# Gathers of a graph kernel held to the matrix engine's steps, and its last stage with logarithm roots and four buffers

## The reference

```python
x = _layernorm(x + _L0_gnn_ref(x, edge_index, edge_attr_16, ...))
x = _layernorm(x + _L1_gnn_ref(src, dst, x, edge_attr_3, ...))
```

```python
d = gelu(layer_norm(gelu(layer_norm(x3 @ Wd1 + bd1)) @ Wd2 + bd2))
logits = w1[target] - w2[source] + d
e = jnp.exp(logits - seg_max[target])
a = e / segment_sum(e, target)[target]
out = segment_sum(a * (w3[source] + d), target)
```

## Time and profile before

| | |
|---|---|
| median of 3 runs | 2032.91 us (2018.93 to 2034.91) |
| the profiled execution | 2048.31 us |
| its span, first to last instruction | 2046.5 us |
| stage dense | about 25 to 720 us |
| stage weigh | about 720 to 870 us |
| stage first | about 870 to 1275 us |
| stage dist | about 1275 to 1413 us |
| stage second | about 1413 to 2046 us |
| granted PE clock, mean of the execution | 0.823 |

### The profile page before, as it was taken

One profiled execution on the slowest core, in us unless ns is written; L12 is line 12 of the kernel. 1 busy time (PEld: TensorE's weight loads), 2 busy tenths in 40 slices (PEclk: granted clock), 3 DMA queues, 4 the chain that ended last, 5 costly groups with the idle time before them and its releaser, 6 DMA issues. The chain is left out here.

```text
span 2046.5 us, 22495 instructions
## 1 busy us (share of the span) xinstructions
PE 1446.2 (71%) x5771; PEld 832.8 (41%) x5771; DVE 1575.8 (77%) x3462; ACT 744.6 (36%) x1570; POOL 1053.9 (51%) x1154
## 2 busy tenths in 40 slices
PE   5787787877788600588888882786777667766773
PEld 4555555555555400133333331674333233333331
DVE  2788777778788668578888783685888888878886
ACT  2676666666677500122322221453211111111111
POOL 3566556666567300025545556002576767776764
PEclk9899898889899755677777775687988988888886
DMA  2455545445555510101111111001211222222120
GB/s 80 129 179 160 163 150 167 150 145 162 161 167 168 120 51 0 38 25 43 42 43 47 41 36 31 4 4 25 46 43 48 44 51 47 48 53 46 48 48 13
DMA packets 163175, 156.87 MB, mean 77 GB/s; under 512 B 84789, under 2 KB 105404, under 8 KB 163049
## 3 DMA queue, kind: packets, MB, share of 16 engines
q1 hardware_dynamic: 131048, 125.34, 20.0%
q0 software_dynamic: 32000, 30.10, 7.6%
HBM read 71.30 MB, written 73.65 MB: 71 GB/s over the span
## 5 line engine op out<-in xcount | busy, mean ns | idle before, releaser
L416 POOL DMA_INDIRECT dense_pairs<-in_x_dram,gix x400 | 418.4, 1046 | 278.9 <-PE bank L460 135.9
L442 PE MATMUL twin<-AC,dense_hb 128*128 128x256 f32 x784 | 219.4, 429 | 93.5 <-DVE dense_hb L594 67.4
L1438 POOL DMA_INDIRECT out_dram<-second_orow,second_stage x200 | 199.5, 998 | 71.1 <-issue 53.2
L1430 POOL DMA_INDIRECT second_pairs<-x_table,second_stage x200 | 203.8, 1019 | 59.2 <-issue 54.4
L954 POOL DMA_INDIRECT x_table<-first_xr,first_stage x200 | 202.3, 1011 | 54.0 <-issue 53.7
L442 PEld LDWEIGHTS twin<-AC,dense_hb 128*128 128x128 f32 x784 | 158.3, 213 | 127.8 <-DVE dense_hb L594 74.8
L948 POOL COPY first_stage<-first_rows 128x4 int32<-128x4 int32 x50 | 10.0, 200 | 310.8 <-DVE first_xr L1148 175.4
L995 PE MATMUL twin<-first_zb,Mstack 128*64 128x512 f32 x400 | 158.9, 885 | 0.0
L1079 DVE TENSOR_TENSOR first_zb<-twin,XT 128x512 f32<-128x512 f32 x200 | 130.8, 686 | 23.1 <-PE twin L987 14.7
L434 PE MATMUL bank<-dense_xT,Mblk 128*128 128x512 f32 x196 | 115.2, 672 | 34.9 <-ACT dense_xT L530 21.7
L987 PE MATMUL twin<-first_wt,headsel 24*128 24x512 bf16 x200 | 74.3, 498 | 81.0 <-DMA first_mask<-mask_rows 37.4
(11 more groups left out here) (270 smaller groups left out, 3603.0 us busy)
## 6 DMA issues: line engine op xcount, KB each, us to landing
dense_rows<-in_x_dram SPq DMA_DIRECT2D x98, 256.0 KB
x_table<-dense_xr SPq DMA_DIRECT2D x98, 256.0 KB
out_dram<-dense_orow SPq DMA_DIRECT2D x98, 256.0 KB
XT<-dense_turned SPq DMA_DIRECT2D x50, 256.0 KB
dense_pairs<-in_x_dram,gix POOLq DMA_INDIRECT x400
target_rows<-first_xr SPq DMA_DIRECT2D x50, 128.0 KB
second_pairs<-target_rows SPq DMA_DIRECT2D x50, 128.0 KB
second_mask<-mask_rows SPq DMA_DIRECT2D x50, 128.0 KB
```

The lines of the kernel that those rows point to most:

```text
L416: pool.indirect_dma_start(out=pairs[b][:, j % 4, F * (j // 4):F * (j // 4) + F], out_offset=None, in_=x, in_offset=bass.IndirectOffsetOnAx ...
L442: last = nc.tensor.matmul(pGC[b][:, j * 256:(j + 1) * 256], hb[b][:, j * 128:(j + 1) * 128], AC[:, :], start=True, stop=True)
L1430: pool.indirect_dma_start(out=pairs[u.off % 2][:, j, 0:F], out_offset=None, in_=x1, in_offset=bass.IndirectOffsetOnAxis(ap=stage[a][:, j:j ...
L1438: pool.indirect_dma_start(out=out, out_offset=bass.IndirectOffsetOnAxis(ap=stage[a][:, 4 + j:5 + j], axis=0), in_=orow[a][:, j, :], in_off ...
```

## The change

In **dense**, each of POOL's gathers now waits for one group of PE: gathers 0 to 3 and 4 to 7 of an edge unit belong to two following slots, and in slot k they wait for `project` of unit k-1, `turn_rows` of unit k, `rows_of_x` of unit k-3 and `rows_of_h` of unit k-2. These are the four groups of PE's slot k, in PE's order.

```diff
+                def after_matmuls(k, part):
+                    if part == 0 and k > 0:
+                        pool.wait_ge(p_made, min(k, DENSE))
+                    if part == 1:
+                        pool.wait_ge(xt_made, min(k + 1, DENSE))
+                    if part == 2 and k > 2:
+                        pool.wait_ge(x_rows_made, min(k - 2, DENSE))
+                    if part == 3 and k > 1:
+                        pool.wait_ge(gc_made, min(k - 1, DENSE))
...
                     for j in range(8):
+                        after_matmuls(2 * e + j // 4, j % 4)
                         pool.indirect_dma_start(
```

```diff
+                    def after_matmuls(u, part):
+                        if part == 0:
+                            atleast(pool, turned, u.count(-1))
+                        if part == 1:
+                            atleast(pool, fell_made, u.count(-2))
+                        if part == 2:
+                            atleast(pool, linear, u.count(-1))
+                        if part == 3:
+                            atleast(pool, rows_made, u.count(-2))
...
+                    def slot(u):
+                        o = u.back(5)
                         for j in range(4):
...
+                            if u.valid(UNITS):
+                                after_matmuls(u, j)
+                                gather(u, j)
+                            if o.valid(UNITS):
+                                if j == 0:
+                                    pool.wait_ge(out_made, o.count(1))
+                                scatter(o, j)
```

```diff
+                    def guess_inverse(u):
...
+                        act.wait_ge(rows_made, u.count(1))
...
+                        nc.scalar.activation(ln_den[:, :, :], sum_rows(u)[:, :, 0, :], ACT.Ln).then_inc(ln_den_made, 1)
...
+                        nc.scalar.activation(inv[:, :, :], ln_den[:, :, :], ACT.Exp, scale=-1.0).then_inc(inv_made, 1)
...
+                    def guess_roots(u):
...
+                        nc.scalar.activation(ve[:, :], s2[:, :], ACT.Identity, bias=eps1[:, :]).then_inc(ve_made, 1)
...
+                        nc.scalar.activation(ln[:, :], ve[:, :], ACT.Ln).then_inc(ln_made, 1)
...
+                        nc.scalar.activation(guess[:, :], ln[:, :], ACT.Exp, scale=-0.5).then_inc(guess_made, 1)
...
+                        nc.scalar.activation(halved[:, :], guess[:, :], ACT.Square, scale=0.5 ** 0.5).then_inc(halves_made, 1)
```

```diff
                     def divide(u):
+
                         dve.wait_ge(inv_made, u.count(1))
+                        atleast(dve, over_made, u.count(0))
+                        nc.vector.tensor_tensor(off[:, :, :], sum_rows(u)[:, :, 0, :], inv[:, :, :], ALU.mult).then_inc(off_made, 1)
+                        nc.vector.tensor_tensor(quo[:, :, :], sum_rows(u)[:, :, 1, :], inv[:, :, :], ALU.mult).then_inc(quo_made, 1)
...
+                        nc.vector.scalar_tensor_tensor(over[:, :, :], off[:, :, :], 2.0, quo[:, :, :], ALU.subtract, ALU.mult)\
+                            .then_inc(over_made, 1)
```

More of the change, by code:

```diff
@@ L1369, in gnn @@
                 sums = [sbp(f"sums{i}", [128, COLS]) for i in range(2)]
-                inv, quo = sbp("inv", [128, 4, F]), sbp("quo", [128, 4, F])
+                ln_den, inv, quo, off, over = (sbp(n, [128, 4, F]) for n in ("ln_den", "inv", "quo", "off", "over"))
                 res, sqr = sbp("res", [128, 4, F]), sbp("sqr", [128, 4, F])
                 cen = [sbp(f"cen{i}", [128, 4, F]) for i in range(2)]
-                orow = [sbp(f"orow{i}", [128, 4, F]) for i in range(2)]
-                mean, nmean, s2 = sbp("mean", [128, 4]), sbp("nmean", [128, 4]), sbp("s2", [128, 4])
@@ L1457, in slot @@
-                        stage_gather(u.back(-1))
-                        if o.valid(UNITS):
-                            scatter(o)
-                    slots(UNITS, 6, slot)
-                    for b in range(2):
-                        pool.wait_ge(scattered[b], 64 * (UNITS // 2))
+                        for j in range(4):
+                            if u.valid(UNITS):
[5 more added lines that the diff above has]
+                                scatter(o, j)
@@ L1465, in _, with sum_rows @@
+                    slots(UNITS, 5, slot)
+                    for b in range(4):
+                        pool.wait_ge(scattered[b], 64 * ((UNITS + 3 - b) // 4))
+                def sum_rows(u):
+                    return pS[:, :].rearrange("p (t s f) -> p t s f", t=4, s=2)
                 @block.tensor
@@ L1493, in falls @@
                         pe.wait_ge(topped, u.count(1))
-                        pe.wait_ge(mask_in[b], u.halves(1) * 32)
+                        pe.wait_ge(mask_in[u.off % 4], u.quarters(1) * 32)
                         atleast(pe, exps_made, u.count(0))
-                        nc.tensor.matmul(pF[:, :], ones[0:1, :], mask[b][0:1, :], start=True, stop=False)
+                        nc.tensor.matmul(pF[:, :], ones[0:1, :], mask[u.off % 4][0:1, :], start=True, stop=False)
                         nc.tensor.matmul(pF[:, :], ident, top[b][:, 0:COLS], start=False, stop=False)
@@ L1544, in slot @@
                     def slot(u):
+                        if u.back(2).valid(UNITS):
+                            guess_inverse(u.back(2))
                         if u.valid(UNITS):
```

183 lines of the change are left out of this document (78 added, 105 removed).

## The result

| | before | changed |
|---|---|---|
| median | 2033.91 us (4 runs, 2018.93 to 2041.67) | 1966.97 us (4 runs, 1964.10 to 1978.06) |
| ratio | | 0.969, interval 0.964 to 0.974 |
| span of the profiled execution | 2046.5 us | 1964.8 us |
| dense, first to last start of L582 / L594 | 665.3 us | 598.8 us |
| second, first to last start of L1563 / L1593 | 581.4 us | 576.8 us |

The change gains 67 us where I forecast 128. Between the spans lie 81.7 us: 66.5 in dense, 4.6 in second, 7.2 behind second's last scan (2046.5 - 2002.8 = 43.7 before, 1964.8 - 1928.3 = 36.5 after), and 3.4 in the rest.

The account below looks back on a forecast made before the run. DVE, busy 77% of the span, was taken as the bound, with PE's late semaphores behind POOL's bursts as loss. -74 - 48 - 6 = -128 from 2048.3 gave 1920, less 15.4 for the median 1905 us; range 1840 to 1985.

Parts of the forecast that it names:

- Dense, -74 us: Stage dense: gathers that wait for PE shorten the slot from 6.86 to 6.1 us, 0.76 x 97 = 74 us saved.
- the signs: What the profile after would show if right, among them "remote" waits in dense below half and second slots near 10.9 us.
- DVE in second, -2.4 us a slot: Stage second: instructions taken from DVE save net 2.4 us a slot, leaving a slot of DVE alone at 8.6 us.
- Second, -48 us: Stage second: the mean slot falls from 11.87 to 10.9 us, over 49 slots 48 us saved.
- rival 3: Second gives nothing, as POOL without a pause keeps PE's increments late and DVE waits instead: 1953 us, chance 0.12.
- POOL's bound of 10.3 us: Stage second: POOL's eight transfers a unit with the pauses between them take 10.3 us, the least a slot can take.
- Four buffers, one gather and one scatter in turn: Stage second: the waits for PE seldom bind, four buffers give a slot to spare, POOL's backlog and late increments remain.
- Start and end, -6 us: Second's last three slots save 3 x 2.4 = 7 us, dense's end may cost 1 to 2: together 6 us saved.

Follow-up runs that it names:

- dense_plain: The kernel before with dense's gathers by POOL replaced by plain loads of as many 256-byte pieces, issued by SP: 1929.9 us beside 2051.67.
- no_scatters: The changed kernel without the scatters of the output rows in stage second: 1821.86 us.
- eight_gathers: The changed kernel with second's scatters replaced by four more gathers a unit into spare buffers: 2009.85 us.
- eight_scatters: The changed kernel with second's gathers replaced by SP's plain loads and each output scattered twice by POOL: 2011.82 us.
- second_alone: The kernel before with everything the change does in second, without the waits in dense: 2051.6 us beside 2053.28, ratio 1.000.
- blocks of four: The changed kernel with POOL's earlier order in second, four gathers in a row, then four scatters: 1859.80 us, ratio 0.986, on a chip without late semaphores.
- tight_turned: The changed kernel with the first gather of a unit in second waiting for the turn of unit u-1 instead of u-2: 1989.22 us beside 2053.28.

## Why the prediction was right or wrong

**Dense, -74 us: right for the chips it was made for.** The slot went from 6.86 to 6.17 us (6.1 forecast), 66.5 us, and the slots of 13 us went but for one at the start (11.92). `dense_plain` (5.74 us) shows that late semaphores were 1.1 of the 1.36 us that I counted as loss, and that they come with POOL's indirect DMAs. The remaining 0.24 us is no loss that they make: without late semaphores every fourth slot takes some 6.55 us and the others 5.5, a mean of 5.74 and not the 5.50 of one smooth slot. They were the right cause, and there are chips without them, where this term is 1 us. Of the signs, the "remote" waits of dense came to half (62.0 of 122.2 us), not below.

**DVE in second, -2.4 us a slot: the work saved is nearly right, its use is not.** DVE's busy time went from 492.7 to 400.0 us, 1.9 us a slot. The sum of single durations gave too much because neighbours overlap: DVE's durations add up to 543.9 us before and 429.4 after, 2.3 us a slot. The slot of DVE alone is 8.62 us where I put 8.6.

**Second, -48 us: the step that failed.** It is "a slot like the 14.35 us one becomes about 12, the short one about 9.5. Mean 10.9". The short slots did become 9 to 10 us, but the long ones did not shrink: 8 slots are above 14 us where 7 were, up to 20.6 instead of 16.4, and the mean is 11.77. The term gave 4.6 us. DVE's 92.7 us less of work became 88 us more of idle time. `no_scatters`, `eight_gathers` and `eight_scatters` show by what: on the same chips the slot is 8.62 us with four transfers a unit, and above 11.7 with eight of any kind. How the waiting comes about is read from traces and not tested: POOL's bursts became longer, single late semaphores too (7.8 us at the scan, and 12.1 in `second_alone`, where 3.6 was the longest), the gathers behind them late for PE, and then POOL waits for DVE and starts its next burst with a backlog. Whether the faster DVE, the buffers or the missing copies of row numbers let the bursts grow stays open. The outcome is that of rival 3, which I gave 0.12, and the end of my range for this term, "nothing, if every us taken from DVE returns as waiting". Its reason holds in part, as DVE's own waits for late semaphores stayed at 60 us. `second_alone` (1.000) shows the outcome without dense.

**POOL's bound of 10.3 us: missed as well, for the changed order.** In blocks of four it is 10.35 us without late semaphores, in turn 11.03, since I took durations from before's blocks for a kernel that alternates. So without late semaphores second would not have gained either: 10.76 before, 11.03 after.

**Four buffers, one gather and one scatter in turn.** I expected both to be neutral. The alternation costs 27 us where POOL is the bound. Whether it costs as much on a chip with late semaphores was not measured, as blocks of four never ran there.

**Start and end, -6 us:** the end gave 7.2 us, where I had put 7.

**The sum.** By the profiled executions rival 3 gives 2048.3 - 80 = 1968.3, and 1966.8 was measured. That its number in the text, 1953, lies 14 us off comes of the 15.4 us that I took off for the median: the changed kernel's profiled execution lay at its median. That the rival's sum comes within 2 us is luck in part: dense gave 66.5 us and not 74, and 4.6 us in second and 3.4 in the rest make it up.

**The rule of the Trainium skill** ("TensorE: Matmul & The Clock Gate", "The cost: per-tile semaphore tail") gives an increment some 26 ns. On the three chips without "remote" waits nothing contradicts it; on the others an increment came 9.4 us late.

## What to carry to other kernels

When a wait ends in "remote" or "issue" long after its maker has finished, look whether POOL was issuing indirect DMAs without a pause. What helped here is fewer of them in a stretch, plain ones from another queue, and a wait that paces POOL where it has time to spare (dense, not second). Moving them to where POOL is idle gave 4% on chips without late semaphores, and was not tried on the others. When POOL or its bursts set the pace, work taken from DVE returns as waiting. Compare on more than one chip before you say what a change is worth: this one was worth 3.1% on one kind and -0.45% on the other.

## What the runs showed of the hardware

- On some chips PE's semaphores, and no other engine's, come late behind POOL's indirect DMAs, 9.4 us late in the slot shown of the changed kernel; on three other chips the same programs show no such wait. The kernel before takes 2034 to 2053 us on the former and 1886 to 1888 us on the latter. What differs stays open, and so does whether it lasts.
- It needs POOL's indirect DMAs without a pause on those chips: four gathers a unit alone (`no_scatters`, POOL pausing up to 5.8 us) show no late semaphore in second, eight with a stop for PE's turn (`tight_turned`) none at DVE, and plain loads of as many bytes by SP none in dense. On a chip without late semaphores 361 in a row bring none.
- A gather of 0.95 us that starts 0.10 us or more into a DVE scan of SBUF operands ends 0.78 us behind the scan (37 of 37 in the changed kernel), up to 1.96 us in all. A scatter that follows a gather takes some 35 ns longer than one that follows a scatter (1.02 us against 0.98).
